# A graph network's layer norm: the residual added on GpSimd, and its projections squared there

## The reference

```python
msg = concat([h[src], h[dst]]) @ Mw.T + Mb
agg = concat([max, min, std, var]) of msg over the arcs of each dst
u = concat([h, agg, agg * amp, agg * att]) @ Uw.T + Ub
u = batch_norm(u * sqrt(1 / N))            # over the nodes
y = leaky_relu(u @ mix_w.T + mix_b, 0.01) + h
h = elu(layer_norm(y) * ln_g + ln_b)       # over the features
```

## Time and profile before

| | |
|---|---|
| time, median of 3 runs | 1845.05 us (1844.66 to 1852.36) |
| time of the profiled execution | 1843.89 us |
| its span, first to last instruction | 1842.0 us |
| GpSimd (POOL) busy | 1242.6 us (67%) |
| VectorE (DVE) busy | 1084.3 us (59%) |
| TensorE (PE) busy | 659.6 us (36%) |
| ScalarE (ACT) busy | 471.1 us (26%) |

### The profile page before, as it was taken

How to read it: one execution, slowest core, us unless ns; L and a number is a source line. 1 busy time by engine, 2 the same in 40 slices (tenths; PEclk the granted TensorE clock), 3 DMA queues, 4 the chain that set the end, 5 groups by cost and what they waited for, 6 DMA issues and landing times.

```text
span 1842.0 us, 9922 instructions
## 1 busy us (share of the span) xinstructions
PE 659.6 (36%) x2106; PEld 382.1 (21%) x2106; DVE 1084.3 (59%) x1972; ACT 471.1 (26%) x1032; POOL 1242.6 (67%) x1344
## 2 busy tenths in 40 slices
PE   6613543333212183533322222162533233221244
PEld 5302322121111041222111111031322121111122
DVE  8824667755565553665655555554666656555544
ACT  0106322222111155222111111046322121111125
POOL 3667777777777607777777777705777777777725
PEclk9956666756666595666666665686766566666677
DMA  7254333433333323333333333313333333333311
GB/s 72 53 156 116 106 105 105 106 106 106 105 106 105 91 85 109 105 105 106 105 105 104 105 104 106 105 61 115 106 105 104 105 105 106 106 106 104 105 33 35
DMA packets 88472, 183.33 MB, mean 100 GB/s; under 512 B 31790, under 2 KB 47489, under 8 KB 88409
## 3 DMA queue, kind: packets, MB, share of 16 engines
q0 software_dynamic: 61264, 164.22, 31.9%
q1 hardware_dynamic: 27150, 18.51, 4.6%
HBM read 169.06 MB, written 14.98 MB: 100 GB/s over the span
## 4 chain that ended last, share of the span: by engine, by line
POOL 48%; issue 19%; DVE 14%; PE 10%; ACT 5%; DMA 2%; SPq 0%; DVEq 0%; POOLq 0%; ACTq 0%
POOL G L551 46%; PE ps L704 3%; DVE ps L1144 2%; PE ps L689 2%; DVE tot L1242 1%; DVE ps L1145 1%; DVE ps L1146 1%; PE ps L701 1%; ACT base L819 1%; POOL rows_by_rank L504 1%; PE ps L642 1%; DVE agg L1244 1%; DVE agg L1246 1%; PE ps L743 1%; DMA G<-p_by_rank,index 1%
## 5 line engine op out<-in xcount | busy, mean ns | idle before, releaser
L551 POOL DMA_INDIRECT G<-p_by_rank,index x812 | 767.8, 946 | 358.3 <-issue 245.5
L1144 DVE TENSOR_TENSOR ps<-ps,G 128x1024 f32<-128x1024 f32 (+3 forms) x255 | 285.7, 1120 | 574.0 <-ACT ps L836 314.7
L551 POOL DMA_INDIRECT G<-p_by_node,index x406 | 384.0, 946 | 130.3 <-issue 120.6
L689 PE MATMUL ps<-wide_ident,agg 128*128 128x128 f32 x300 | 83.7, 435 | 943.4 <-ACT agg L849 943.4
L704 PE MATMUL ps<-w_u_sb,aggT 128*128 128x384 f32 x600 | 289.9, 642 | 0.0
L689 PEld LDWEIGHTS ps<-wide_ident,agg 128*128 128x128 f32 x300 | 53.7, 217 | 958.9 <-ACT agg L849 958.9
L704 PEld LDWEIGHTS ps<-w_u_sb,aggT 128*128 128x128 f32 x600 | 163.4, 272 | 150.9 <-issue 76.4
L842 ACT ACTIVATE msq<-tot,rdeg 128x128 f32<-128x128 f32 x75 | 30.1, 401 | 589.7 <-DVE tot L1242 537.2
L1146 DVE TENSOR_TENSOR ps<-ps,G 128x512 f32<-128x512 f32 (+3 forms) x255 | 161.9, 635 | 0.0
L1145 DVE TENSOR_TENSOR ps<-ps,G 128x512 f32<-128x512 f32 (+3 forms) x255 | 161.8, 634 | 0.0
L701 PE MATMUL ps<-w_own,hT 128*128 128x384 f32 x150 | 111.6, 847 | 0.0
(11 more groups left out here) (206 smaller groups left out, 1130.0 us busy)
## 6 DMA issues: line engine op xcount, KB each, us to landing
G<-p_by_rank,index POOLq DMA_INDIRECT x812, 2.7
G<-p_by_node,index POOLq DMA_INDIRECT x406, 2.8
p_by_rank<-base SPq DMA_DIRECT2D x12, 512.0 KB, 2.9
p_by_node<-G SPq DMA_DIRECT2D x6, 514.0 KB, 4.7
w_u_sb<-in_w_u SPq DMA_DIRECT2D x3, 768.0 KB
x_r<-rows_by_rank SPq DMA_DIRECT2D x1, 1600.0 KB, 8.1
windows<-src_pad SPq DMA_DIRECT2D x1, 1118.0 KB, 24.8
index<-rows_by_rank SPq DMA_DIRECT2D x1, 468.0 KB
```

Of the source, the lines that this page charges most:

```text
L551: g.indirect_dma_start(G[:, n % R, j, 0:w], None, table, bass.IndirectOffsetOnAxis(ap=index[:, t, k0 + j:k0 + j + 1], axis=0))\
L689: ins = nc.tensor.transpose(ps[:, 2, i * D:(i + 1) * D], agg[:, t % 2, i * D:(i + 1) * D], ident[:, :])
L1144: TT(run[:, 0:nk, :], run[:, 0:nk, :], G[:, n % R, 0:nk, 0:2 * D], ALU.add)
```

## The change

In stage B of layers 0 and 1, GpSimd (`stage_b`, new) adds `hT` to the mixed rows in place (`residual`), once `leaked` has come, and signals `residual_in`; TensorE's `centre_rows` waits for that and makes one product in place of two. GpSimd also squares the projections (`squares`), and ScalarE does not. GpSimd's order is: residual(0), (1), (2), then squares(s - 3) and residual(s) by turns, and squares(4), (5), (6) last; then it goes on to the gathers. `p_copied` is now signalled by GpSimd, so SyncE's stores and the next layer's `bases` wait for it. The last layer keeps its two products.

```diff
+        residual_in = Signal(sem("residual_added"), NC)
...
+            def residual(l, c):
+                mixed_in = cb[:, 0, c % 2, 0:CH[c][1] * D]
+                pool.wait_ge(leaked.sem, leaked.at(l, c + 1))
+                g.tensor_tensor(mixed_in, mixed_in, hT[:, cols(c)], ALU.add).then_inc(residual_in.sem, 1)
+
+            def squares(l, c):
+                t0, nt = CH[c]
+                pool.wait_ge(p_added.sem, p_added.at(l, c + 1))
+                p = base[:, t0:t0 + nt, TOP, :]
+                g.tensor_tensor(base[:, t0:t0 + nt, SQR, :], p, p, ALU.mult).then_inc(p_copied.sem, 1)
+
+            def stage_b(l):
+                for s in range(NC + 3):
+                    if s >= 3:
+                        squares(l, s - 3)
+                    if s < NC:
+                        residual(l, s)
...
                 gather(l)
+                if l < L - 1:
+                    stage_b(l)
...
-                mm(ps[:, 2 + c % 2, 0:w], centre[:, :], hT[:, cols(c)], start=True, stop=False)
-                pe.wait_ge(leaked.sem, leaked.at(l, c + 1))
-                mm(ps[:, 2 + c % 2, 0:w], centre[:, :], cb[:, 0, c % 2, 0:w], start=False,
+                if l == L - 1:
+                    mm(ps[:, 2 + c % 2, 0:w], centre[:, :], hT[:, cols(c)], start=True, stop=False)
+                    pe.wait_ge(leaked.sem, leaked.at(l, c + 1))
+                    mm(ps[:, 2 + c % 2, 0:w], centre[:, :], cb[:, 0, c % 2, 0:w], start=False,
+                       stop=True).then_inc(centred.sem, 1)
+                    return
+                pe.wait_ge(residual_in.sem, residual_in.at(l, c + 1))
+                mm(ps[:, 2 + c % 2, 0:w], centre[:, :], cb[:, 0, c % 2, 0:w], start=True,
                    stop=True).then_inc(centred.sem, 1)
...
-                    if s >= 3 and next_layer:
-                        project(l, s - 3)
```

## The result

| | before | after |
|---|---|---|
| time, median | 1844.86 us (4 runs) | 1876.19 us (4 runs, 1872.5 to 1879.55) |
| ratio, 95% interval | 1 | 1.0161 (1.0127 to 1.0194) |
| profiled execution, and its span | 1843.89, 1842.0 us | 1872.5, 1870.7 us |
| first mix product to first gather, behind layer 0 and layer 1 | 38.58, 38.58 us | 51.87, 52.12 us |

The kernel became slower by 31 us, 28.6 between the two profiled executions. Of these 26.8 lie in the two stretches of the last row, which I call the stretch from here on: it starts with the first mix product of stage B and ends with the first gather of the next layer.

A forecast was written before the change was run, and what follows sets the result against it. GpSimd's gathers were taken to bound the run, with stage B's hole between them on the path; 6.9 - 0.35 + 6.0 = 12.6 us a layer, 25.2 in two, on 1843.9 gave 1869 us, range 1852 to 1878.

The forecast's parts named there:

- The stretch between the gathers: Stage B between two layers' gathers: GpSimd issues none for 55.72 us, so any time added there lengthens the run equally.
- The product removed: TensorE's first centring product, 0.86 us a chunk, fills a wait for the leaky relu; removing it gains next to nothing.
- A: GpSimd's residual add between leaky relu and centring product: 1.2 us plus 0.1 us handing over, 1.3 us in all.
- The rivals that need a cheap add: Engines overlap and the add is near 0.83 us: 1853 us, chance 0.13; an actual gain needs A under about 0.2 us.
- 6.6: Lengthening of a layer in us if both engines ran freely: 6.9 for the longer chain, less 0.35 for the squares.
- 0.35 shorter: End phase, squares moved off ScalarE: 0.5 us saved, 0.15 us added by GpSimd's last squares, together - 0.35 a layer.
- The two engines run one after the other: GpSimd's square and VectorE's elu and leaky relu exclude each other: 5 x 1.2 = 6.0 us a layer.
- The fifth 1.2: End phase: the square of chunk 4 against the elu of chunk 5 costs 1.2 us once more.
- the costly end: Of the bounds 0 and 6.0 us a layer for GpSimd beside VectorE, the 6.0 one, which the forecast took.
- TensorE's clock: Rival: TensorE, less busy, falls to 1.2 GHz, 2.67 us more a step, + 32 us, 1901 us; chance 0.07.
- the serial case: Square and VectorE's instructions one after the other: centring products some 6.9 us apart, 1869 us; chance 0.52.
- the overlapping one: Rival: the engines don't hold each other, only the chain lengthens: steps 5.7 us, + 13.2, 1857 us; chance 0.26.

The follow-up runs named there:

- e5: Kernel before without the product of the layer's input in layers 0 and 1, nothing in its place; 1.0078 of the kernel before, stretch 41.0 and 40.5 us.
- e8: Changed kernel with residual ahead of squares on GpSimd and the removed product kept, its result unread; 1.0128 of the kernel before, stretch 48.3 and 47.1 us.
- e2: Changed kernel with only the squares on GpSimd, centring by two products as before; 1.0073 of the kernel before, stretch 40.3 and 40.3 us.
- e3: Changed kernel with GpSimd's order turned round, residual ahead of the squares; 1.0165 of the kernel before, stretch 53.7 and 51.1 us.
- e6: Changed kernel with mix, bias, leaky relu and residual one step ahead in layers 0 and 1; 1.0059 of the kernel before, stretch 39.9 and 39.7 us.
- e4: Changed kernel with the removed product put back into a bank that nothing reads; 1.0115 of the kernel before, stretch 49.4 and 48.4 us.
- e1: Changed kernel with the squares back on ScalarE, only the residual on GpSimd; 1.0176 of the kernel before, stretch 53.5 and 53.2 us.
- r1: Changed kernel run again without edit on chip 11; 1.0164 of the kernel before, stretch 54.96 and 55.15 us.
- e7: Changed kernel with squares on ScalarE, and mix to residual one step ahead in layers 0 and 1; 1.0070 of the kernel before, stretch 40.4 and 39.6 us.

## Why the prediction was right, and where only by its sum

The forecast was 1869 us in a range of 1852 to 1878, and the median is 1876. Direction and size hold. Point by point:

- **The stretch between the gathers is on the path one for one: right.** 26.8 of the 28.6 us are there.
- **The product removed is worth next to nothing: right.** e5 shows it by itself, 4.44 us a step against 4.39. It is worth less than nothing through the clock, which the sum left out.
- **A = 1.3 us for the residual: right.** The add takes 1.26 us, with the handing over 1.34 (e8 against the earlier trace rows); the price was taken from a select's row by its rate, so its nearness is in part luck. The rivals that need a cheap add fall with it. The estimate of 1.12 us for the add, a quarter of the figure in the Trainium skill (GPSIMD Engine Reference, Performance versus the Vector engine), is a little low here. In sum, though, e8 is 8.5 to 9.7 us over before, not 6.6. In layer 0 one slow distance at the start is part of it (6.53 us). In layer 1 the product of chunk 0 is later by 0.3 to 0.4 us more than A (5.10 us behind the first mix, 3.37 to 3.53 before). And in both layers the end phase takes 10.7 to 10.9 us, where I had it 0.35 shorter than 10.0; about 0.8 of that is the held elu.
- **The two engines run one after the other: right in kind, wrong in size.** This is the term that was mis-sized: "the square's 1.2 us comes on the chain in chunks 3, 4 and 5, in chunk 6, and once more in the end phase", 5 x 1.2 = 6.0 us a layer. The hold is shown by e2 (leaky relu 1.2 us only beside a square), e3 (0.69 with the order turned round, and the hold on L1354 instead) and e6 (elu 1.57). But it costs 0.52 us a step, not 1.2. The square alone takes 1.04 and not 1.2; it begins while the elu is under way and waits 0.4 of it, not all; and the instruction that was held ends 0.55 us behind the other's end, not its whole 0.75. The fifth 1.2, in the end phase, did not come at all in the changed kernel, where the elu of chunk 5 starts first and the square is the one that waits. Over a stretch the hold is 1.6 us in e2, and by the estimate below some 2 in the changed kernel. The Trainium skill (SBUF — State Buffer, Who interferes with whom) has it that a VectorE instruction with two SBUF inputs contends with a GpSimd instruction that reads SBUF, and one with at most one SBUF input, outside certain fast modes, does not; the leaky relu, the elu and L1351 agree. That the one that comes second is blocked for the whole of the other's instruction doesn't come out of these rows in full: in e6 some 0.2 us ran beside it. L1354, with one tile, was held too, so two tiles are not needed for it.
- **An argument for the costly end was a wrong sum.** "2.4 us of GpSimd within the 2.3 us from 672.50": from 672.50 to the leaky relu's end at 673.95 and 1.3 for the residual are 2.75 us, so square and residual would have fitted. In the changed kernel GpSimd waits 0.63 us between them, for the held leaky relu.
- **TensorE's clock: a rival at 0.07, and it is in the result.** I took it as all or nothing, 32 us if every step ran at 1.2 GHz, and held against it the end phase with 0.90. It fell for part of the stage: 0.70 in the first 17 us, and 0.55 in just that end phase, which is 1.1 us longer than e4's. Where steps are slow, one takes 1.66 us more (7.45 against 5.79, e1 and e3), not the 2.67 that I had. The changed kernel's stretch of 52.0 is 3.1 us over e4's mean of 48.9, so the clock is some 6 us of the 27 in the first comparison, and by r1's 55.1 us it is 6 us a layer, 12 in all, on chip 11.

The parts, as an estimate, from the layers of e8 and e4 that have no slow first distance (47.1 and 48.4 us, with 0.8 of e8's counted as hold): 38.6 before, 7.7 for the residual, 2.1 for the hold, 3.6 for the clock, together 52. The forecast had 6.6, 6.0 and 0. It came out near because a cost taken too high made up for two that were too low; that is luck, and the 1876 us inside the range don't prove the sum. What I said would show the serial case, steps of 6.9 us, did not come (6.3); nor did the 5.7 of the overlapping one.

Open: in which step the clock falls. It isn't the same in the two layers of one run, and idle time alone doesn't set it: the changed kernel has steps of 6.3 us with TensorE busy 3.71 us of them at a granted clock of 1.00. I have no edit that sets it other than giving TensorE work. The pauses of the gather stage weren't looked into.

## What to carry to other kernels

An instruction that an engine gets through while a chain of the same length runs on others is free; taking it away gains nothing, and here it cost granted clock. What replaces it on that chain costs its whole length and its handing over. Ask of an offload first whether the chain that it joins has slack. Doing that chain a step earlier makes some, and took the wait out of the steps here (e7), though the stage as a whole became no shorter. And check in the rows which VectorE instructions run beside the moved work: those with two SBUF operands were held here, and so was one with a single tile (L1354).

## What the runs showed of the hardware that I had not expected

- TensorE with idle time in each step in some layers lost the granted clock for part of a stage (0.70 and 0.79 against 1.00), and steps went from 5.78 to 7.45 us. One product more a step, 0.86 us that nobody reads, kept all steps from chunk 2 on at the high clock in both layers of e4 and e8, and the stretch is shorter by 3 us a layer or more.
- GpSimd adds two float32 tiles of 128x512 in 1.26 us, and squares one, given as both inputs, in 1.04.
- An instruction that is held by the other engine shows as a long one, not as idle time: the leaky relu's 1.22 us have no wait in front that names GpSimd. A row that is longer in some chunks than in others is what to look for.
